# Self-attention of a decoder layer on one core: the order of copies and high parts, the place of the table steps, and the place of P's transposes are changed

## The chip, the cores and the metric

One core of one Trainium2 chip. The time is the device time of one execution in microseconds; before the change it was 1856.21 us, the median of three runs (1848.88 to 1856.5).

## The reference

A decoder layer on x (16 batches of 112 rows, 1024 wide) and a context (16 x 375 x 1024), float32: self-attention, cross-attention and a feed-forward part with 4-bit weights, each followed by a residual sum and a layer norm.

```python
# self-attention (width d = 256)
qkv = einsum('bsc,cf->bsf', x, Wqkv) + bqkv;  q, k, v = split(qkv)
attn = softmax(einsum('bqd,bkd->bqk', q, k) * d ** -0.5)
x = layernorm(x + einsum('bqd,dc->bqc', einsum('bqk,bkd->bqd', attn, v), Wo) + bo)
# cross-attention
Q = x @ Wq.T + bq;  K = ctx @ Wk.T + bk
x = layernorm(x + softmax(Q @ K.T / 32) @ ctx)
# feed-forward: W[k, n] = scales[g_idx[k], n] * (w4[k, n] - (z4[g_idx[k], n] + 1))
x = layernorm(x + (silu(x @ Wg) * (x @ Wu)) @ Wd)
```

## The kernel before

The kernel is written with one instruction list for each engine and hand-made semaphores; an engine takes its list in order, and a wait in it holds all that stands behind. Large products are made in float16 with a high and a low part of each operand: three passes (high x high, high x low, low x high). A high part is a scaled copy by ScalarE, a low part is the rest, by VectorE (GpSimd in some stages).

**Self-attention** (the first 255 us of the span) goes over 4 groups of 4 batches (rows 0 to 3 below, b in the code; S = 112 tokens each, a group is 448 columns). For a group g TensorE does, in order: four products for q and k (f = 0 to 3, 24 matmuls of 448 columns each, L1646 to L1650, into two banks of PSUM, so product f waits for the copy of f - 2); v of row 0 (24 matmuls of 256 columns); the scores of all four rows; v of rows 1, 2, 3; the transposes of P (L1671) when P is ready; the first half of the transposes of the next group's x (L1621); P times v; the second half; and the output product row by row. All products have the helper's line, L1628. In group 0 products 0 and 1 are L1641.

ScalarE copies q and k out of PSUM with scale and bias (L1356). From group 1 on the high part of the last row of the group before (`x1_hi`, L1350) stands between the copies of products 0 and 1; the high parts of rows 0 to 2 of a group stand at the group's end, so row 2's is ahead of the next group's copy of product 0. `x1_hi` waits for the normalised row and for the store of the slot's earlier row (two slots, stored by SP at L2045). Then come the exponentials (L1366), the high parts of the next x (L1344) and of the output's left operand (L1373).

VectorE: `x_max` of the next group (L490), the low part of the last row (L469), the group's entry of `beside`, then the maximum of the scores (L536), `x_factor` of the next group (L505 to L508, behind GpSimd's all-reduce L1154, which waits for `x_max`), the scaling of P (L543, L545), the two copies of v (L549, two rows each), the copy of P transposed (L554), low parts, and for each row the residual sum (L577), statistics and normalisation (L475).

The `beside` entries are the **table steps** for the feed-forward part: `table_rows` in group 1 (index rows, then numbers of rows and masks, L597 to L631), `table_parts` in group 2 (L636 to L666, scales split into three bfloat16 parts and zeros unpacked) and `select` in group 3 (L674 to L677). They are small steps with a semaphore wait after each. SP stores the tables (12 DMAs, L2093 to L2100) ahead of its part for the last group, and the selection (L2133) behind the first context's loads.

**Weight product** (about 240 to 351 us): M = Wq' Wk, 8 chunks of 32 float32 matmuls of 512 columns, 13.8 us each. ScalarE copies each chunk (L1401) and issues the load of the weights for a later one (L1400); GpSimd makes the bias terms (L1200 to L1210). TensorE's `largest_of_context(0)` (L1725) stands behind the sixth chunk. VectorE meanwhile: clears the padding of both context slots (L876), the maxima of context 0 (L772), `context_largest(0)` (L782, which waits for L1725), context 0's factor, the largest of m (L870), context 0's low parts (L803, behind ScalarE's high parts L1418), the maxima of context 1, the rest of m (L870), and, behind GpSimd's all-reduce L1242, the factors and low parts of M (L910), to which TensorE's L1810 is tied. SP's `next_ctx(1)` (L2117) waits for context 0's low parts; behind it stand the transposes of x1 and context 0 that cross-attention reads. The selection and the index rows lie in the memory of context slot 1.

Of the kernel before, what the change touches and what calls it, by code (L numbers as in the profile page):

```python
# [35 lines left out]
P = 128  # L36
# [4 lines left out]
def decoder_layer(nc, t_in, out):  # L41
    x_d, ctx_d = t_in["x"], t_in["ctx_4096"]
    NB, S, D = x_d.shape
# [7 lines left out]
    GB = 4  # L51
# [38 lines left out]
    with ExitStack() as ctx:  # L90
# [311 lines left out]
        def known(n, limit):  # L402

            return isinstance(n, int) and n < limit
# [38 lines left out]
        def _(dve):  # L443
# [82 lines left out]
            def self_attention(g, more, beside=()):  # L526
# [26 lines left out]
                dve.wait_ge(s_pt, g + 1)  # L553
                dve.tensor_copy(pt[0:S, :, :], bk[4][0:S, 0:TG].rearrange("p (b k) -> p b k", b=GB)).then_inc(s_pte, 1)  # L554
# [38 lines left out]
            def table_rows():  # L593
# [11 lines left out]
                T["idx"] = steps[0]  # L605

# [136 lines left out]
            self_attention(2, True, (table_parts,))  # L743
            self_attention(NG - 1, False, (select,))
# [130 lines left out]
            for i in range(2):  # L875
                dve.memset(cxp[i][96:P, CC - 1, :, :], 0.0)  # L876
# [4 lines left out]
            context_largest(0)  # L881
            context_factor(0, 0, False)
# [454 lines left out]
        def _(act):  # L1337
# [14 lines left out]
            def self_attention(g, more):  # L1352
                act.wait_ge(s_gf, 5 * g + 5)
                for f in range(2 * HC):
# [3 lines left out]
                    if f == 0 and not known(g, 1):  # L1358
                        x1_hi(g * GB - 1, GB - 1, 2 * g)
# [16 lines left out]
                for b in range(GB - 1):  # L1376
                    x1_hi(g * GB + b, b, 2 * g + b // 2 + 1)
# [232 lines left out]
        def _(pe):  # L1610
# [22 lines left out]
            def self_attention(g, more):  # L1633
# [30 lines left out]
                for b in range(1, GB):  # L1664
                    mm = v_rows(b)
                    if b % 2:
                        mm.then_inc(s_v, 1)
# [4 lines left out]
                mm.then_inc(s_pt, 1)  # L1672
                if more:
                    transposed_rows(g + 1, range(4))
# [334 lines left out]
        def _(sp):  # L2009
# [80 lines left out]
            sp.wait_ge(s_t, T["parts"])  # L2090
            for k in range(3):
                for m in range(2):
                    sp.dma_start(tabr_d[m, k * GU:(k + 1) * GU, :].rearrange("g n -> (g n)").rearrange("(p c) -> p c", p=P),  # L2093
                                 parts[:, k, at_fl[m]:at_fl[m + 1]]).then_inc(s_tabo, 16)
                sp.dma_start(dtab_d[k * GD:(k + 1) * GD, :].rearrange("g n -> (g n)").rearrange("(p c) -> p c", p=P),
                             parts[:, k, at_fl[2]:]).then_inc(s_tabo, 16)
            for m in range(2):
                sp.dma_start(tabr_d[m, 3 * GU:, :].rearrange("g n -> (g n)").rearrange("(p c) -> p c", p=64),
                             z_bf[0][64 * m:64 * m + 64, :]).then_inc(s_tabo, 16)
# [304 lines left out]
```

## Time and profile before

| | before |
|---|---|
| median of 3 runs, us | 1856.21 (1848.88 to 1856.5) |
| profiled execution, us | 1853.36 |
| its span, us | 1851.6 |
| TensorE busy | 1742.2 us, 94% |
| VectorE busy | 1064.8 us, 58% |
| ScalarE busy | 494.2 us, 27% |
| GpSimd busy | 500.9 us, 27% |

The span runs from the first to the last instruction; what the execution's time has beyond it lies around the program. A timeline lists instructions merged by line: start, duration, line, operation, shapes, count, and in brackets how long the engine was idle before and what released it. PE is TensorE, DVE VectorE, ACT ScalarE, POOL GpSimd, SPq the DMA queue of SyncE. Some matmul records are missing from the trace.

### The profile page before, as it was taken

To read this page: it belongs to the slowest core of one execution; us is meant where nothing else is said; L and a number is where in the kernel's file an instruction comes from. 1 tells how busy PE (TensorE), PEld (TensorE's weight loads), DVE (VectorE), ACT (ScalarE), POOL (GpSimd) and SP (SyncE) were. 2 spreads that over 40 slices of the span, in tenths; PEclk is the share of its full clock that TensorE was granted. 3 is DMA by queue.
4 is the path that set the end of the run, shared out by engine and by line. 5 is a ranking of instruction groups with operands and counts; after the bars stand their busy time and mean duration, and the time that the engine had idled before them with its cause. 6 is when DMAs were issued, how large, how long until landed. Compare 5 with 4: busy or idle time off the path is not lost.

```text
span 1851.6 us, 26675 instructions
## 1 busy us (share of the span) xinstructions
PE 1742.2 (94%) x9784; PEld 981.6 (53%) x9784; DVE 1064.8 (58%) x1656; ACT 494.2 (27%) x734; POOL 500.9 (27%) x326
## 2 busy tenths in 40 slices
PE   5898899898999969998999999999999899999998
PEld 3666644496787844444444444444445344444443
DVE  7788550666888856567778777777775111111011
ACT  3222210354555533232323223233232100000000
POOL 0322378223333425543322323223231000000000
PEclk9999999999999989999999999999999999999999
DMA  9342561599999975764231231322313822122120
GB/s 324 99 132 80 158 205 34 121 213 234 233 240 231 248 160 127 168 148 88 49 95 47 66 77 47 94 48 56 87 45 75 324 104 107 53 106 106 53 106 23
DMA packets 335590, 231.89 MB, mean 125 GB/s; under 512 B 288224, under 2 KB 302624, under 8 KB 333348
## 3 DMA queue, kind: packets, MB, share of 16 engines
q1 hardware_dynamic: 329284, 227.85, 47.2%
q10 hardware_dynamic: 6240, 3.15, 0.6%
q8 instruction: 43, 0.70, 0.2%
q14 instruction: 23, 0.19, 0.0%
HBM read 122.93 MB, written 60.83 MB: 99 GB/s over the span
## 4 chain that ended last, share of the span: by engine, by line
PE 47%; issue 27%; DVE 10%; DMA 6%; SPq 5%; POOL 2%; ACT 1%; DVEq 0%; POOLq 0%; ACTq 0%
PE psum L1628 45%; SPq L2143 4%; DMA arena<-arena 3%; DMA arena<-in_x 2%; DVE arena L803 1%; POOL small L1149 1%; POOL arena L1158 1%; PE psum L1839 1%; PE psum L1857 1%; DVE arena L974 1%; DVE arena L972 1%; DVE arena L969 1%; DMA x_parts_scratch<-arena 1%; DMA arena<-in_L_xattn_Wq 1%; DVE arena L993 1%
## 5 line engine op out<-in xcount | busy, mean ns | idle before, releaser
L1628 PE MATMUL psum<-arena 128*128 128x448 f16 (+5 forms) x7176 | 1276.7, 339 | 51.8 <-DMA arena<-arena 21.1
L1628 PEld LDWEIGHTS psum<-arena 128*128 128x128 f16 (+2 forms) x7176 | 753.6, 109 | 556.3 <-issue 97.2
L1967 PE MATMUL psum<-arena 128*128 128x512 f16 x1820 | 393.5, 379 | 6.2 <-DMA arena<-down_weights_scratch 3.7
L1967 PEld LDWEIGHTS psum<-arena 128*128 128x128 f16 x1820 | 177.6, 98 | 222.1 <-DMA arena<-down_weights_scratch 5.4
L1263 POOL TENSOR_TENSOR arena<-arena 128x1024 f16<-128x1024 f32 (+1 forms) x60 | 149.8, 2509 | 430.5 <-ACT arena L1494 430.5
L1131 DVE SCALAR_TENSOR_TENSOR arena<-psum,small,arena 128x512 f32<-128x512 f32 x28 | 20.9, 750 | 331.8 <-PE psum L1967 331.8
L1149 POOL TENSOR_TENSOR small<-small 112x1 f32<-112x1 f32 (+1 forms) x46 | 50.9, 1106 | 503.7 <-DVE small L464 503.7
L1494 ACT ACTIVATE arena<-arena 128x1024 f16<-128x1024 f32 (+1 forms) x60 | 68.8, 1173 | 128.2 <-DVE arena L955 99.8
L1508 ACT ACTIVATE arena<-arena,small 128x448 f32<-128x448 f32 x68 | 45.5, 668 | 208.6 <-DVE arena L1061 145.2
L1223 POOL TENSOR_TENSOR arena<-arena 128x224 f16<-128x224 f32 x64 | 54.8, 857 | 119.7 <-ACT arena L1412 119.6
L953 DVE TENSOR_TENSOR arena<-arena,psum 128x1024 f32<-128x1024 uint32 x65 | 79.1, 1217 | 2.9 <-PE psum L1839 0.9
L955 DVE TENSOR_TENSOR arena<-arena,psum 128x1024 f32<-128x1024 f32 x65 | 79.3, 1221 | 2.2
L1517 ACT ACTIVATE arena<-arena 128x448 f16<-128x448 f32 (+1 forms) x88 | 50.7, 576 | 106.8 <-DVE arena L982 106.8
L993 DVE TENSOR_TENSOR arena<-arena 128x448 f16<-128x448 f32 (+1 forms) x88 | 57.7, 656 | 36.8 <-ACT arena L1517 36.8
L772 DVE TENSOR_REDUCE small<-arena 128x1 f32<-128x1024 f32 (+1 forms) x48 | 57.6, 1215 | 25.4 <-DMA arena<-in_ctx 25.2
L803 DVE SCALAR_TENSOR_TENSOR arena<-arena,small 128x1024 f16<-128x1024 f32 (+1 forms) x48 | 61.2, 1278 | 12.0 <-ACT arena L1418 12.0
L1418 ACT ACTIVATE arena<-arena,small 128x1024 f16<-128x1024 f32 (+1 forms) x48 | 51.8, 1138 | 47.8 <-DVE small L799 47.8
L459 DVE BATCH_NORM_STATS2 small<-arena 112x6 f32<-112x512 f32 (+1 forms) x92 | 58.8, 681 | 1.4 <-DVE small L799 1.1
L982 DVE SCALAR_TENSOR_TENSOR arena<-arena,small 128x448 f32<-128x448 f32 (+1 forms) x72 | 48.9, 680 | 13.4 <-ACT arena L1526 10.6
L475 DVE TENSOR_SCALAR arena<-arena,small 112x1024 f32<-112x1024 f32 (+1 forms) x46 | 40.4, 878 | 26.4 <-POOL small L1149 26.4
L1270 POOL TENSOR_TENSOR arena<-arena 128x1024 f16<-128x1024 f32 x21 | 44.8, 2133 | 39.9 <-ACT arena L1502 39.9
L933 DVE TENSOR_TENSOR arena<-arena,small 128x1024 uint32<-128x1024 uint32 x43 | 53.7, 1249 | 0.3
(213 smaller groups left out, 1208.5 us busy)
## 6 DMA issues: line engine op xcount, KB each, us to landing
h_scratch<-arena SPq DMA_DIRECT2D x84, 224.0 KB, 2.9
arena<-h_scratch SPq DMA_DIRECT2D x13, 1376.0 KB, 6.1
arena<-in_ctx SPq DMA_DIRECT2D x32, 512.0 KB, 5.3
arena<-in_x SPq DMA_DIRECT2D x32, 448.0 KB, 5.6
x_scratch<-arena SPq DMA_DIRECT2D x32, 448.0 KB, 3.4
arena<-x_scratch SPq DMA_DIRECT2D x32, 448.0 KB, 4.6
arena<-in_L_ffn_down_qweight SPq DMA_DIRECT2D x21, 512.0 KB
down_weights_scratch<-arena SPq DMA_DIRECT2D x20, 512.0 KB, 3.8
```

The costliest lines, as they stand in the source:

```text
L459: dve.bn_stats(st[0:n, 6 * h:6 * h + 6], y[:, h * HALF:(h + 1) * HALF]).then_inc(s_st, 1)
L772: ins = dve.tensor_reduce(cmx[0:CP[c], c:c + 1], cx[0:CP[c], c, :], AX.X, ALU.max, apply_absolute_value=True)
L803: dve.scalar_tensor_tensor(cxp[b % 2][0:CP[c], c, 1, :], cx[0:CP[c], c, :], fc[0:CP[c], b:b + 1], cxp[b % 2][0:CP[c], c, 0, :], ALU.mult, ...
L953: dve.tensor_tensor(w, w.bitcast(U32), zeros, ALU.subtract).then_inc(s_dq, 1)
L955: dve.tensor_tensor(w, w, scales, ALU.mult).then_inc(s_wf if done is None else done, 1)
L993: dve.tensor_tensor(h_st[0:n, 1, cols], h_f[0:n, :], h_st[0:n, 0, cols], ALU.subtract).then_inc(s_hl, 1)
L1149: pool.tensor_tensor(rstd[0:n, :], ve[0:n, :], mhalf[0:n, :], ALU.pow).then_inc(s_rstd, 1)
L1263: return pool.tensor_tensor(dst[:, :, 1, :], wf32[:, lo * HALF:hi * HALF].rearrange("p (c n) -> p c n", n=P), dst[:, :, 0, :], ALU.subtract)
L1494: return act.activation(wgu[s][:, lo * 4:hi * 4, 0, :], wf32[:, lo * HALF:hi * HALF].rearrange("p (c n) -> p c n", n=P), ACT.Identity)
L1628: mm = pe.matmul(out, a, r, start=(k == 0), stop=(k == len(pairs) - 1))
L1967: mm = pe.matmul(bk[2 * s + c], ht[s][:, i, a, :], weights_of(i, w, c), start=(i == 0 and (w, a) == PASSES[0]), stop=(i == NI - 1 and (w, ...
L2143: sp.dma_start_transpose(cxt[s].rearrange("p l k t -> p (l k) t")[:, :, c * P:(c + 1) * P], cxp[s][:, c, :, :].rearrange("p l d -> p (l d) ...
```

## The change

Four edits, all of order: (1) ScalarE's high parts of rows 2 and 3 stand behind the copies of products 0 and 1 of the next group, in the groups that have one; in the last group rows 0 to 2 stay where they were. (2) TensorE transposes P behind v of row 2, ahead of v of row 3; VectorE copies P transposed between its two copies of v. (3) `table_rows` is cut in two; its first part stays in group 1, its second part (`row_numbers`), `table_parts` and `select` go behind `context_largest(0)`, and the clearing of context slot 1 goes behind them. (4) SP's table stores go behind the first context's loads and the last row's store, ahead of the store of the selection. No computation is added or removed.

```diff
@@ -550,8 +550,10 @@
-                dve.wait_ge(s_pt, g + 1)
-                dve.tensor_copy(pt[0:S, :, :], bk[4][0:S, 0:TG].rearrange("p (b k) -> p b k", b=GB)).then_inc(s_pte, 1)
+                    if p == 0:
+                        dve.wait_ge(s_pt, g + 1)
+                        dve.tensor_copy(pt[0:S, :, :], bk[4][0:S, 0:TG].rearrange("p (b k) -> p b k", b=GB)
+                                        ).then_inc(s_pte, 1)
@@ -603,6 +605,8 @@
                 T["idx"] = steps[0]
+
+            def row_numbers():
@@ -740,8 +744,8 @@
             self_attention(1, True, (table_rows,))
-            self_attention(2, True, (table_parts,))
-            self_attention(NG - 1, False, (select,))
+            self_attention(2, True)
+            self_attention(NG - 1, False)
@@ -872,13 +876,17 @@
-            for i in range(2):
-                dve.memset(cxp[i][96:P, CC - 1, :, :], 0.0)
+            dve.memset(cxp[0][96:P, CC - 1, :, :], 0.0)
             factor_step(dve.memset(cmx, 0.0))
             factor_step(dve.memset(cmx[:, CC:], LOW))
             for c in range(CC):
                 context_max(0, c)
             context_largest(0)
+            row_numbers()
+            table_parts()
+            select()
+
+            dve.memset(cxp[1][96:P, CC - 1, :, :], 0.0)
             context_factor(0, 0, False)
@@ -1355,8 +1363,8 @@
-                    if f == 0 and not known(g, 1):
-                        x1_hi(g * GB - 1, GB - 1, 2 * g)
+                    if f < 2 and not known(g, 1):
+                        x1_hi(g * GB - 2 + f, GB - 2 + f, 2 * g)
@@ -1373,7 +1381,7 @@
-                for b in range(GB - 1):
+                for b in range(GB - 2 if more else GB - 1):
                     x1_hi(g * GB + b, b, 2 * g + b // 2 + 1)
@@ -1661,15 +1669,14 @@
                 mm.then_inc(s_s, 1)
-                for b in range(1, GB):
-                    mm = v_rows(b)
-                    if b % 2:
-                        mm.then_inc(s_v, 1)
+                v_rows(1).then_inc(s_v, 1)
+                v_rows(2)
                 pe.wait_ge(s_p, g + 1)
                 pe.wait_ge(s_ve, 2 * g + 1)
                 for b in range(GB):
                     mm = pe.transpose(bk[4][0:S, b * S:(b + 1) * S], pr[0:S, b, :], ident[0:S, 0:S])
                 mm.then_inc(s_pt, 1)
+                v_rows(3).then_inc(s_v, 1)
                 if more:
                     transposed_rows(g + 1, range(4))
                 pe.wait_ge(s_pte, g + 1)
@@ -2087,6 +2094,36 @@
             sp.dma_start(idx_w, idx_d[2 * D:].partition_broadcast(P)).then_inc(s_tin[1], 16)
+            self_attention(NG - 1, False, False)
...
+            next_ctx(0)
+            store_parts(NB - 1, (NB - 1) % 2)
             sp.wait_ge(s_t, T["parts"])
             for k in range(3):
                 for m in range(2):
@@ -2099,36 +2136,6 @@
                          z_bf[1]).then_inc(s_tabo, 16)
-            self_attention(NG - 1, False, False)
...
-            next_ctx(0)
-            store_parts(NB - 1, (NB - 1) % 2)
             sp.wait_ge(s_t, T["sel"])
```

## Rows read from the trace of the kernel before

**Rows 1.** TensorE's timeline, 40 to 260 us: start, duration, line, operation, count [idle before <- releaser]

```profile
63.80 0.57 PE L1671 MATMUL psum<-ident,arena 112*112 112x112 f32 x4 [1.85 <-DVE arena L549]
...
94.78 22.87 PE L1628 MATMUL psum<-arena 128*128 128x448 f16 x160 [4.54 <-ACT arena L1356]
...
117.86 1.95 PE L1621 MATMUL psum<-ident,arena 112*128 112x112 f32 x16
...
172.39 0.59 PE L1671 MATMUL psum<-ident,arena 112*112 112x112 f32 x4 [3.67 <-DVE arena L549]
...
172.82 3.01 PE L1621 MATMUL psum<-ident,arena 112*128 112x112 f32 x16
...
201.31 4.71 PE L1628 MATMUL psum<-arena 128*128 128x448 f16 x24 [0.99 <-ACT arena L1356]
...
207.22 16.77 PE L1628 MATMUL psum<-arena 128*128 128x448 f16 x136 [1.20 <-ACT arena L1356]
```

**Rows 2.** ScalarE's timeline, 60 to 420 us

```profile
93.05 1.06 ACT L1350 ACTIVATE arena<-arena 112x1024 f16<-112x1024 f32 x1 [4.86 <-DMA x_parts_scratch<-arena]
```

**Rows 3.** VectorE's timeline, 40 to 270 us

```profile
61.39 0.15 DVE L505 TENSOR_SCALAR small<-small 128x1 f32<-128x1 f32 x1 [4.28 <-POOL small L1154]
...
114.33 0.62 DVE L545 TENSOR_TENSOR arena<-arena,small 112x448 f32<-112x448 f32 x1
...
150.03 4.41 DVE L490 TENSOR_REDUCE small<-arena 112x1 f32<-112x4096 f32 x1
...
167.73 0.62 DVE L536 TENSOR_REDUCE small<-psum 112x4 f32<-112x448 f32 x1
...
170.35 1.32 DVE L545 TENSOR_TENSOR arena<-arena,small 112x448 f32<-112x448 f32 x1
```

**Rows 4.** GpSimd's timeline, 60 to 420 us

```profile
109.26 0.38 POOL L1154 PARTITION_ALL_REDUCE small<-small  x1 [11.29 <-issue]
...
160.81 0.82 POOL L1154 PARTITION_ALL_REDUCE small<-small  x1 [11.55 <-issue]
...
168.86 2.33 POOL L1158 TENSOR_TENSOR arena<-arena 112x1024 f32<-112x1024 f32 x1 [7.22 <-issue]
...
328.01 1.90 POOL L1200 TENSOR_TENSOR arena<-arena,small 128x1024 f32<-128x1024 f32 x1 [4.61 <-DMA arena<-in_L_xattn_Wq]
...
334.88 2.35 POOL L1210 TENSOR_TENSOR arena<-arena 128x1024 f32<-128x1024 f32 x1
```

**Rows 5.** VectorE's timeline, 216 to 375 us

```profile
324.01 0.29 DVE L782 TENSOR_REDUCE small<-psum 128x1 f32<-128x128 f32 x1 [57.89 <-PE psum L1725]
...
339.92 3.67 DVE L803 SCALAR_TENSOR_TENSOR arena<-arena,small 128x1024 f16<-128x1024 f32 x3 [9.46 <-ACT arena L1418]
...
350.54 2.27 DVE L870 TENSOR_REDUCE small<-arena 128x1 f32<-128x2048 f32 x1
```

**Rows 6.** Windows of VectorE: stretch, length, busy (instructions), clock, DMA share, GB/s

```profile
155.40:167.73 12.33, 10.57 (x43) 1.00 0.00 1
...
106.53:111.70 5.17, 3.88 (x30) 1.00 0.02 3
...
sum 20.46, DVE 17.20; mean DVE 5.73
```

**Rows 7.** SP's queue, timeline of DMA issues, 60 to 400 us

```profile
211.21 0.90 SPq L2093 DMA_DIRECT2D table_scratch<-arena  x2
...
216.76 0.58 SPq L2100 DMA_DIRECT2D down_table_scratch<-arena  x1
...
259.59 8.78 SPq L2135 DMA_DIRECT2D arena<-down_table_scratch  x1
```

**Rows 8.** DMA view of the stretch 254 to 272 us, its line of packets

```profile
DMA packets 5870, 5.06 MB, mean 281 GB/s; under 512 B 2982, under 2 KB 5030, under 8 KB 5869
```

**Rows 9.** TensorE's timeline, 250 to 420 us

```profile
268.56 55.20 PE L1628 MATMUL psum<-arena 128*128 128x512 f32 x128 [1.68 <-DMA arena<-in_L_xattn_Wq]
...
358.66 5.96 PE L1810 MATMUL psum<-arena 128*128 128x224 f16 x30 [3.30 <-DVE arena L910]
```

More of the change, by code:

```diff
@@ L2089, in _ @@
             sp.dma_start(idx_w, idx_d[2 * D:].partition_broadcast(P)).then_inc(s_tin[1], 16)
[L2090 to L2099, printed above, removed]
-            sp.dma_start(dtab_d[3 * GD:, :].rearrange("g n -> (g n)").rearrange("(p c) -> p c", p=P),
-                         z_bf[1]).then_inc(s_tabo, 16)
             self_attention(NG - 1, False, False)
@@ L2131, in _ @@
             store_parts(NB - 1, (NB - 1) % 2)
+            sp.wait_ge(s_t, T["parts"])
+            for k in range(3):
+                for m in range(2):
+                    sp.dma_start(tabr_d[m, k * GU:(k + 1) * GU, :].rearrange("g n -> (g n)").rearrange("(p c) -> p c", p=P),
+                                 parts[:, k, at_fl[m]:at_fl[m + 1]]).then_inc(s_tabo, 16)
+                sp.dma_start(dtab_d[k * GD:(k + 1) * GD, :].rearrange("g n -> (g n)").rearrange("(p c) -> p c", p=P),
+                             parts[:, k, at_fl[2]:]).then_inc(s_tabo, 16)
+            for m in range(2):
+                sp.dma_start(tabr_d[m, 3 * GU:, :].rearrange("g n -> (g n)").rearrange("(p c) -> p c", p=64),
+                             z_bf[0][64 * m:64 * m + 64, :]).then_inc(s_tabo, 16)
+            sp.dma_start(dtab_d[3 * GD:, :].rearrange("g n -> (g n)").rearrange("(p c) -> p c", p=P),
+                         z_bf[1]).then_inc(s_tabo, 16)
             sp.wait_ge(s_t, T["sel"])
```

## The prediction

> **What bounds the kernel now.** Read the timeline of TensorE over self-attention first. It is nearly solid, so the time of this stage is its work plus the few gaps. The change aims at these: 4.54 us ahead of group 1's third q/k product, 0.99 and 1.20 us in group 3, both behind ScalarE's copy L1356, and 3.67 us ahead of group 2's transposes of P [rows 1]. ScalarE's timeline says why the first is there: the high part of row 2 (L1350) stands ahead of the copy, and itself waited 4.86 us for the store of row 0 [rows 2]. VectorE's timeline says why the last is there: in group 2 the maximum of the scores (L536) begins only at 167.73, behind the table steps [rows 3], though the scores were ready near 161 (v's products ended at 172.39 - 3.67 = 168.7, and three of them, 7.8 us, stand behind the scores). That gap costs more than its length: after it 16 transposes took 3.01 us, where 1.95 is usual [rows 1], as TensorE was granted 1.2 GHz there instead of 2.4.
>
> Then read what P itself needs. After the maximum VectorE takes `x_factor`, whose L505 waits for GpSimd's all-reduce: in group 0 for 4.28 us, to 61.39 [rows 3]. In groups 1 and 2 the all-reduce begins at 109.26 and 160.81 [rows 4], in group 2 6.4 us after x_max ended (L490, 150.03 and 4.41 us [rows 3]). It is hidden now, and is what is late next.
>
> Times below are on the clock of the trace before; a shift is carried to the next group, as each group starts behind the normalisation of the last one.
>
> **Copies ahead of high parts.** Nothing is added. The copy of product 0 no longer stands behind row 2's high part, nor that of product 1 behind row 3's. Products 2 and 3 then run without a gap. In group 3 this is 0.99 + 1.20, about **-2.1 us**: P waits for no all-reduce there, and the new order of v's products is neutral (the copy of P is hidden, but v's last copy now ends where P's did). In groups 1 and 2 the all-reduce cuts the gain short, next.
>
> **P transposed inside v's products.** The same matmuls in another order. One row's v is 24 of them, about 2.6 us (136 in 16.77 less 24 in 4.71 leaves 12.1 for four rows of v and some 1.6 of scores [rows 1]). Before, three rows of v covered the softmax; now two do (5.2 us), and the third comes after the transposes of P, ahead of the next group's x transposes. If L505 is the late one, x transposes begin at L505 + 2.4 (61.39 to 63.80 in group 0 [rows 1, 3]) + 0.4 for P's transposes + 2.6 for v = L505 + 5.4.
> - Group 0: L505 stays at 61.39, as nothing ahead of it moved. TensorE was through with v at 63.80 - 1.85 = 61.95; it is now through with two rows of it at 59.3, waits 4.4 us and starts the x transposes at 66.8 instead of 64.2: **+2.6**. The gap of 3.67 was followed by the low clock, that of 1.85 was not; v's last row then runs partly at half speed, about **+1.5**. Bounds of both together 2.6 and 5.2; +4.1.
> - Group 1: scores near 104, table rows to 106.5 (their second half begins there [rows 6]), L505 at 109.26 + 0.38, x transposes at 115.1 against 117.86: -2.75. The new gap of 2.9 us lies between the two above; I take half of 1.5 for the clock: **-2.0** (bounds -1.25, -2.75).
> - Group 2: the table steps are gone, scores near 157.5, L505 at 160.81 + 0.4, x transposes at 166.7 against 172.8: -6.1, and the 1.1 us of slow transposes goes: **-7.2** (bounds -6, -7.6).
>
> **Table steps moved.** They go behind `context_largest(0)`. VectorE's long idle stretch in the weight product, 57.89 us, ends *in* that step: L782 waits for TensorE's L1725, which comes behind six of eight chunks, and runs at 324.01 [rows 5]. VectorE takes its queue in order, so the moved steps begin at 324.3, after the hole and not in it. What is left behind it is 9.46 us ahead of L803 [rows 5]. Into this go `row_numbers` (5.17), `table_parts` (12.33) and `select`, 20.46 together [rows 6], and the memset that now stands behind `select`, about 1.1 (estimate). 21.5 - 9.46 = **+12.0**. Queued behind these steps are context 0's factor and low parts and the maximum of m on VectorE, ScalarE's high parts and the copy of the last chunk, and SP's load of context 1.
>
> Beside them GpSimd adds and multiplies from 328.01 to 337.23 [rows 4]. The scaling of P (L545) took 1.32 us instead of 0.62 while GpSimd's add of 168.86 ran, and ended 0.5 us after it [rows 3, 4]: a wide VectorE step with both inputs in SBUF waited for it. The wide table steps would begin at 331.9. Let each wait for the GpSimd step then running and GpSimd take its next one in between: the three scalings start near 332.1, 332.9 and 335.1 and the first cast behind GpSimd's last step near 337.8, where it would be 333.0: **+4.8**. Bounds 0 (no wide step meets one) and 7 (GpSimd's work left at 330, all of it waited for).
>
> The Trainium skill, "SBUF — State Buffer", section "SBUF: two separate sides", speaks against this placement: it has an exclusive lock for the whole instruction between GpSimd and a VectorE step with two SBUF inputs. By that rule `table_parts`' one-column products wait too, which no row shows; the turns would then cost 5.5 us instead of 4.8, and the forecast would be 0.7 us later.
>
> **SP's queue.** The 12 table stores (211.21 to 217.34, 6.1 us [rows 7]), the store of the selection, the wait for all 12, the loads of tab_d and two residual loads now all lie ahead of `next_ctx(1)`. With parts ready near 346.5, the stores are issued by 352.6 and the selection's by 353.3, the last table store lands near 356 (estimate), and context 1 is issued near 358, when L803 (from 356.7) frees it anyway. The residual loads (448 KB each) are new ahead of it in the DMA engines, 3.2 us at 281 GB/s [rows 8]; of that I count **+0.9** beyond the 6.9 us from L803's end to the last maximum of context 1 (343.6 to 350.5 [rows 5]), as the rest fits between its three loads. But tab_d's load once held SP for 8.78 us behind the selection's store [rows 7], with 1.5 MB of context queued ahead of both; now only the store is. Bounds 0 and 5.3 us.
>
> From the maxima of context 1 on the chain is as before: maximum of m, all-reduce, factors, high part, and TensorE at 358.66, which now waits far longer than 3.30 us for it [rows 9]. TensorE's L1725 for context 1 and the small products of v2 and u also come behind these maxima now; they fit beside the 8.1 us that follow.
>
> **One gain on the side.** SP's store of the selection (704 KB) leaves the stretch in which ScalarE's first load of weights is on its way, for which TensorE waits 1.68 us [rows 9]. It was 2.5 us of traffic [rows 8]: **-1.7** (bounds 0, -1.7).
>
> **The sum.** +4.1 - 2.0 - 7.2 - 2.1 - 1.7 = -8.9 up to the end of the weight product; +12.0 + 4.8 + 0.9 = +17.7 behind it; net +8.8. The profiled execution took 1853.36 us (span 1851.6, and 1.8 around it), 2.9 under the median of the three runs, 1856.21, and inside their spread. Forecast: 1853.4 + 8.8 = **1862.2 us**.
>
> **Rivals.**
> 1. *SP's queue becomes the bound.* tab_d's load holds it as before, to 353.3 + 8.8 = 362.1; context 1 then lands about 4.5 us later: 1866.7. With the clock losses of groups 0 and 1 in full (+1.8) and the full 7 us of turns (+2.2) it would be 1870.7. For it: the 8.78 row. Against: less is queued ahead. It decides from the point where tab_d is issued later than 358. Chance 0.2.
> 2. *The turns with GpSimd are nearly free*, as the wide steps fall between its instructions: 4.8 us less, 1857.4; with the better bounds of groups 0 and 1 (-2.3), 1855.1. For: GpSimd works for 9 us only. Against: the L545 row. Chance 0.25.
> 3. *The moved steps cost nothing*, because what TensorE waits for at 358.66 isn't VectorE's chain, or because they run in the hole after all: only the gains are left, 1853.4 - 8.9 = 1844.5. For: VectorE is idle for most of the weight product. Against: the hole ends in L782, ahead of them in the queue. Chance 0.08.
>
> The forecast itself has 0.47. What a measurement of this kernel can tell from no change is about 0.5%, 9.3 us, and the forecast lies at that edge: half of its chance is put on each side. Faster 0.08; slower 0.20 + half of 0.47 = 0.44; same the rest, 0.48. The range goes from 1850 (case 2 with every gain at its best) to 1871.
>
> **What would show it.** Group 0: a gap of 4.4 us ahead of P's transposes and a low clock after it. Groups 1 and 2: no gap behind L1356, gaps of 2.9 and 0.8 us ahead of P's transposes, with L505 waiting for GpSimd. The gap ahead of the third chunk of the weight product gone. VectorE: table steps directly behind L782, no idle time ahead of L803. TensorE: 15 to 25 us of gaps between the weight product and the first product with M, with small products in them. I am wrong if these are under 8 us, if L782 runs before TensorE's six chunks are done, or if group 0 does not lose.

## The result and the profile after

| | before | after |
|---|---|---|
| median, us | 1854.07 (6 runs, 1848.88 to 1856.5) | 1866.44 (6 runs, 1862.27 to 1869.69) |
| profiled execution, us | 1853.36 | 1865.75 |
| its span, us | 1851.6 | 1864.0 |

The changed kernel takes 1.0067 times as long, with an interval of 1.0047 to 1.0087: 12.4 us slower. The forecast was 1862.2, with a range of 1850 to 1871. One later execution of the kernel before took 4698.54 us, in the slow state, and is left out of the median that e8_residual_late and e10_both_behind are set against.

From here on lines are those of the changed kernel. The ones that matter have moved: L1628 to L1636 (products), L1671 to L1677 (P's transposes), L1621 to L1629 (x transposes), L1725 to L1732 (the context's small transposes), L1810 to L1817 (first product with M), L782 to L786, L803 to L807. A fence of an experiment has that kernel's own line numbers.

Read TensorE first, as before. Its timeline over self-attention and the weight product, as in [rows 1, 9]:

```profile
64.19 0.96 PE L1677 MATMUL psum<-ident,arena 112*112 112x112 f32 x4 [4.64 <-DVE arena L549]
64.95 3.97 PE L1636 MATMUL psum<-arena 128*112 128x256 f16 x24
68.75 1.93 PE L1629 MATMUL psum<-ident,arena 112*128 112x112 f32 x16
...
82.90 30.39 PE L1636 MATMUL psum<-arena 128*112 128x512 f16 x196 [0.89 <-DVE arena L579]
114.47 0.59 PE L1677 MATMUL psum<-ident,arena 112*112 112x112 f32 x4 [1.18 <-DVE arena L549]
114.90 2.79 PE L1636 MATMUL psum<-arena 128*112 128x256 f16 x24
117.52 1.94 PE L1629 MATMUL psum<-ident,arena 112*128 112x112 f32 x16
...
163.40 0.60 PE L1677 MATMUL psum<-ident,arena 112*112 112x112 f32 x4 [1.31 <-DVE arena L549]
...
166.45 1.94 PE L1629 MATMUL psum<-ident,arena 112*128 112x112 f32 x16
...
218.42 93.11 PE L1636 MATMUL psum<-arena 128*112 128x512 f16 x240 [1.44 <-DVE arena L561]
311.37 0.38 PE L1732 MATMUL psum<-ident,small 128*128 128x128 f32 x2
...
360.08 0.77 PE L1732 MATMUL psum<-ident,small 128*128 128x128 f32 x2 [20.86 <-DVE small L781]
360.64 3.41 PE L1748 MATMUL psum<-ones,arena 128*128 128x1 f32 x16
...
369.03 0.73 PE L1817 MATMUL psum<-arena 128*128 128x224 f16 x6 [1.08 <-DVE arena L918]
```

The waits for ScalarE's copies are gone: each group is one run of products from 82.90, 131.70 and 180.63 on. The price of P's new place stands in group 0: 4.64 us idle, then a row of v in 3.97 us where 2.79 is usual. The x transposes begin at 68.75; before, 64.20 (63.80 and the four transposes ahead [rows 1]). In group 2 they begin at 166.45 instead of 172.82. At the weight product's sixth chunk TensorE is 12.2 us ahead (311.37, before 323.59). Then come 20.86 us without a product, and the first product with M starts at 369.03, 10.4 us *later* than the 358.66 of [rows 9].

VectorE's timeline behind the weight product, which answers to [rows 5, 6]:

```profile
311.79 0.29 DVE L786 TENSOR_REDUCE small<-psum 128x1 f32<-128x128 f32 x1 [56.64 <-PE psum L1732]
...
317.14 0.81 DVE L640 TENSOR_SCALAR small<-small 128x3 f32<-128x3 f32 x1
...
321.09 1.75 DVE L653 TENSOR_TENSOR small<-small 128x1 f32<-128x1 f32 x1
...
323.06 2.98 DVE L658 TENSOR_SCALAR arena<-arena,small 128x172 f32<-128x172 f32 x3
...
344.99 3.68 DVE L807 SCALAR_TENSOR_TENSOR arena<-arena,small 128x1024 f16<-128x1024 f32 x3
355.34 1.22 DVE L776 TENSOR_REDUCE small<-arena 128x1 f32<-128x1024 f32 x1 [6.67 <-DMA arena<-in_ctx]
```

and GpSimd beside it, as in [rows 4]:

```profile
316.03 1.90 POOL L1208 TENSOR_TENSOR arena<-arena,small 128x1024 f32<-128x1024 f32 x1 [4.20 <-DMA arena<-in_L_xattn_Wq]
...
320.93 1.89 POOL L1215 TENSOR_TENSOR arena<-arena,small 128x1024 f32 x1 [0.21 <-POOL arena L1213]
322.90 2.35 POOL L1218 TENSOR_TENSOR arena<-arena 128x1024 f32<-128x1024 f32 x1
```

The hole of VectorE (56.64 us) still ends in the step ahead of the moved ones, and there is no idle time ahead of L807 any more. Between the two lie the table steps, 20.5 us of them in [rows 6], in part stretched by turns with GpSimd: L640 ends at 317.95 and GpSimd's L1208 at 317.93; L653 ends at 322.84, L1215 at 322.82. L658's three instructions take 2.98 us, where 0.99 is their time without GpSimd. The last term is on the right of the last line: context 1 lands 6.67 us after VectorE was ready for it.

### The profile page after: what moved, and what is told of

Same layout as the page of the kernel before. It is cut to its first block, busy times and chain, and to the rows that moved or that the text cites. A ratio compares the mean times of both kernels' runs of the same rounds, so it can differ in the third digit from the quotient of the medians.

```text
span 1864.0 us, 26676 instructions
## 1 busy us (share of the span) xinstructions
PE 1745.0 (94%) x9784; PEld 983.9 (53%) x9784; DVE 1067.9 (57%) x1656; ACT 493.9 (26%) x734; POOL 499.1 (27%) x326
## 3 DMA queue, kind: packets, MB, share of 16 engines
q10 hardware_dynamic: 6240, 3.15, 0.6%
## 4 chain that ended last, share of the span: by engine, by line
PE 48%; issue 28%; DVE 10%; SPq 5%; DMA 5%; POOL 2%; ACT 1%; DVEq 0%; POOLq 0%; ACTq 0%
PE psum L1636 46%; SPq L2150 4%; DMA arena<-arena 3%; DMA arena<-in_x 1%; DVE arena L807 1%; PE psum L1846 1%; PE psum L1864 1%; POOL small L1157 1%; DVE arena L982 1%; DVE arena L980 1%; POOL arena L1166 1%; DVE arena L977 1%; DVE arena L1001 1%; DVE arena L918 1%; DVE arena L483 1%
## 5 line engine op out<-in xcount | busy, mean ns | idle before, releaser
L1636 PE MATMUL psum<-arena 128*128 128x448 f16 (+5 forms) x7176 | 1275.9, 339 | 41.2 <-DMA arena<-arena 23.1
L1636 PEld LDWEIGHTS psum<-arena 128*128 128x128 f16 (+2 forms) x7176 | 754.6, 109 | 543.4 <-issue 93.7
L1139 DVE SCALAR_TENSOR_TENSOR arena<-psum,small,arena 128x512 f32<-128x512 f32 x28 | 20.9, 751 | 331.9 <-PE psum L1974 331.9
L807 DVE SCALAR_TENSOR_TENSOR arena<-arena,small 128x1024 f16<-128x1024 f32 (+1 forms) x48 | 61.2, 1279 | 2.6 <-ACT arena L1426 2.5
L990 DVE SCALAR_TENSOR_TENSOR arena<-arena,small 128x448 f32<-128x448 f32 (+1 forms) x72 | 48.9, 680 | 13.4 <-ACT arena L1534 10.6
L941 DVE TENSOR_TENSOR arena<-arena,small 128x1024 uint32<-128x1024 uint32 x43 | 53.7, 1249 | 0.3
L1166 POOL TENSOR_TENSOR arena<-arena 112x1024 f32<-112x1024 f32 x16 | 39.9, 2494 | 51.8 <-issue 27.7
```

Of the source, the lines that this page charges most:

```text
L807: dve.scalar_tensor_tensor(cxp[b % 2][0:CP[c], c, 1, :], cx[0:CP[c], c, :], fc[0:CP[c], b:b + 1], cxp[b % 2][0:CP[c], c, 0, :], ALU.mult, ...
L1166: pool.tensor_tensor(xr[0:S, b % 2, :], xr[0:S, b % 2, :], bo_b[0:S, :], ALU.add).then_inc(s_xb, 1)
L1636: mm = pe.matmul(out, a, r, start=(k == 0), stop=(k == len(pairs) - 1))
```

## The experiments

Ten kernels ran. Two places of each trace sum them up: when TensorE reaches L1732 (so what self-attention cost), and how long it is from there to the first product with M. The median is set against the median of the kernel before in the same session (1852.57 for e1, e2, e4 and e6; 1854.31 for e3, e5, e7 and e9; 1852.63 for e8 and e10; 1854.07 for the changed kernel). In the diffs of this section most context is cut, and what stands in brackets is told in words.

| kernel | L1732 at | from there to L1817 | median, against before |
|---|---|---|---|
| before | 323.59 | 35.1 | |
| after | 311.37 | 57.7 | 1866.44, +12.4 |
| e1_hole | 313.50 | 35.0 | 1844.03, -8.5 |
| e5_tables | 317.21 | 57.3 | 1871.83, +17.5 |
| e6_ctx_first | 310.04 | 53.9 | 1862.52, +10.0 |
| e8_residual_late | 315.19 | 53.7 | 1863.01, +10.4 |
| e3_copies | 325.27 | 35.3 | 1853.65, -0.7 |
| e4_ptrans | 336.38 | 35.1 | 1862.18, +9.6 |
| e2_both_orders | 340.16 | 34.9 | 1869.51, +16.9 |
| e9_p_behind_v | 306.48 | 34.8 | 1835.78, -18.5 |
| e7_factor_behind_p | 305.00 | 35.0 | 1833.41, -20.9 |
| e10_both_behind | 305.70 | 35.1 | 1834.85, -17.8 |

The first column is from single executions, and differs by some us between executions of the same instructions; e8_residual_late shows where. The trace of e4_ptrans is of an execution of 1869.03 us, 6.9 above that kernel's median, those of e3_copies and e2_both_orders lie 4.8 and 2.9 above theirs; so these three first-column entries are high.

### Behind the weight product

**e1_hole**: the changed kernel, with the table steps ahead of the step that waits, so that they can use the hole.

```diff
+            row_numbers()
+            table_parts()
+            select()
+            dve.memset(cxp[1][96:P, CC - 1, :, :], 0.0)
             context_largest(0)
-            row_numbers()
-            table_parts()
-            select()
-            dve.memset(cxp[1][96:P, CC - 1, :, :], 0.0)
             context_factor(0, 0, False)
```

> The changed kernel with row_numbers, table_parts and select (and the clearing of context slot 1) ahead of context_largest(0) instead of behind it. Theory (the steps cost time only because they stand behind the wait for TensorE's sixth chunk): they run in VectorE's 57 us hole, the gap behind the weight product goes back to about 3 us, the 12.2 us gained up to its end stay: 22.6 us less than the changed kernel, 1843.8 us. Rival (what the steps cost is shared use with GpSimd and the DMA engines, wherever they stand in the weight product): GpSimd's bias steps and ScalarE's weight loads behind them slip, TensorE waits in the weight product, and half or more of the 22.6 us stays: 1852 us or more.

Measured: 1844.03 us, 0.9954 (0.9936 to 0.9971). Its VectorE timeline:

```profile
273.29 5.71 DVE L658 TENSOR_SCALAR arena<-arena,small 128x172 f32<-128x172 f32 x3
...
287.84 7.37 DVE L665 TENSOR_SCALAR arena<-arena 128x43 uint32<-128x43 uint32 x8
...
315.87 0.29 DVE L786 TENSOR_REDUCE small<-psum 128x1 f32<-128x128 f32 x1
...
329.83 3.68 DVE L807 SCALAR_TENSOR_TENSOR arena<-arena,small 128x1024 f16<-128x1024 f32 x3 [7.51 <-ACT arena L1426]
```

The whole loss behind the weight product, 22.6 us, is gone (35.0 against before's 35.1), with not a step less on VectorE. So it was the place of the steps in the queue, and TensorE's wait was for this chain. The hole was only just long enough: GpSimd is busy for 51.95 of the 58 us from 257 to 315, and the steps, 20.5 us in [rows 6], lasted from 257.34 to 314.95. L786 had been waiting for 2 us by then.

**e5_tables**: the kernel before, with the table steps and SP's stores moved as in the change, and the other two parts undone. The diff is against the changed kernel.

```diff
-                    if f < 2 and not known(g, 1):
-                        x1_hi(g * GB - 2 + f, GB - 2 + f, 2 * g)
+                    if f == 0 and not known(g, 1):
+                        x1_hi(g * GB - 1, GB - 1, 2 * g)
...
-                for b in range(GB - 2 if more else GB - 1):
+                for b in range(GB - 1):
...
-                v_rows(1).then_inc(s_v, 1)
-                v_rows(2)
+                for b in range(1, GB):
+                    mm = v_rows(b)
+                    if b % 2:
+                        mm.then_inc(s_v, 1)
                 [P's transposes; VectorE's copy of P goes back behind both copies of v]
-                v_rows(3).then_inc(s_v, 1)
```

> The kernel before with the table steps and SP's stores moved as in the change (behind context_largest(0)), both other orders undone. Theory: group 2 loses its 3.7 us gap and the low clock, 5.2 us; the weight load's 1.7 us go; the 22.6 us behind the weight product come: 15.7 us slower than before, 1868 us. Rival (most of the gain in self-attention comes from the table steps, about 9 us, as they also hold P in groups 1 and 3): 1864 us.

Measured: 1871.83 us, 1.0107 (1.008 to 1.0135), 17.5 us slower than before, where the theory had 15.7. Its part in self-attention is a gain of 6.4 us, its loss behind the weight product 22.2 us (57.3 against 35.1), as in the changed kernel. The tables alone are worse than the whole change: the two new orders, which come with a loss in the kernel before (below), take back 5 us once the tables are gone from self-attention.

**e6_ctx_first** and **e8_residual_late** ask what holds context 1's load. The first puts it ahead of the store of the selection, of tab_d and of the residual loads; the second moves only the residual loads.

```diff
+            next_ctx(1)                      # e6 only
             sp.wait_ge(s_t, T["sel"])
             sp.dma_start(seld_d ...)
             ...
-            for n in range(2):               # e8 only: behind next_ctx(1)
-                load_residual(n, n)
-            next_ctx(1)                      # e6 only
+            for n in range(2):               # e8 only
+                load_residual(n, n)
```

> The changed kernel with SP's load of context 1 ahead of the store of the selection, the loads of tab_d and the residual loads. Theory (context 1 landed 4.3 us late because 1.8 MB were ahead of it in the DMA engines, SP itself was free): VectorE's idle time ahead of context 1's maximum goes from 6.67 to about 2 us, 4.3 us less than the changed kernel, 1862 us. Rival (the landing is bound otherwise, as all of the traffic shares the engines in any order): 1866 us, same as the changed kernel.

> The changed kernel with only the two residual loads (448 KB each) put behind the load of context 1; the selection's store and tab_d's loads stay ahead. Theory (the 0.9 MB of residual rows were half of the 1.8 MB ahead of context 1): the 6.67 us wait ahead of context 1's maximum goes to about 4, 2.5 us less than the changed kernel, 1864 us. Rival (the store of the selection with its pieces of 256 bytes was what held the DMA engines): no change, 1866.5 us.

Measured: 1862.52 us, 1.0063 (1.0041 to 1.0084), and 1863.01 us, 1.0055 (1.0035 to 1.0075). By the medians this is 3.9 and 3.4 us less than the changed kernel, and 2.4 and 2.0 us less when each is set against the kernel before of its own session; the intervals overlap, so the traces have to carry it. SP's queue in the changed kernel, and the landing times of the DMA view from 340 to 360 us (issues, KB each, us from issue to landing):

```profile
340.78 0.43 SPq L2140 DMA_DIRECT2D down_selection_scratch<-arena  x1
342.10 1.84 SPq L2142 DMA_DIRECT2D arena<-down_table_scratch  x1
...
344.60 0.80 SPq L2104 DMA_DIRECT2D arena<-x_scratch  x2
346.31 1.55 SPq L2112 DMA_DIRECT2D arena<-in_ctx  x2
```

```profile
arena<-in_ctx SPq DMA_DIRECT2D x2, 512.0 KB, 9.3
arena<-x_scratch SPq DMA_DIRECT2D x2, 448.0 KB, 7.6
down_selection_scratch<-arena SPq DMA_DIRECT2D x1, 704.0 KB, 4.9
```

SP issued the context at 346.31, when the first of L807's three instructions was just through: nobody waited for SP. The load then took 9.3 us to land, where it took 4.5 us before. Ahead of it had gone the 704 KB of selection, which had landed by then (340.78 and 4.9), and the 896 KB of residual rows, issued at 344.60 and 7.6 us on their way. With the context first, or with the residual loads behind it, it lands in 4.6 and 4.2 us, and VectorE's wait for it shrinks from 6.67 us to 1.14 and 1.09 us. One line of each kernel:

```profile
348.59 1.22 DVE L776 TENSOR_REDUCE small<-arena 128x1 f32<-128x1024 f32 x1 [1.14 <-DMA arena<-in_ctx]
```

```profile
353.86 1.22 DVE L776 TENSOR_REDUCE small<-arena 128x1 f32<-128x1024 f32 x1 [1.09 <-DMA arena<-in_ctx]
```

A part of this comes back in the waits for the later pieces of context 1: all three waits together go from 7.41 us to 3.59 and 3.21. From L1732 to the first product with M both kernels save some 4 us. As moving the residual loads alone does it, and as SP issues the context 1.3 to 1.4 us behind L807's start in all three kernels, these 896 KB in the DMA engines are the cause, not SP's queue and not tab_d. The selection's store stays ahead in e8_residual_late and costs nothing that shows.

e8_residual_late also shows why single executions scatter. Its self-attention is the changed kernel's, and yet it reaches L1732 3.8 us later. The difference lies in a step that normalises x, and comes once in group 0 and once in group 1:

```profile
87.68 2.83 DVE L475 TENSOR_SCALAR arena<-arena,small 112x1024 f32<-112x1024 f32 x1 [0.45 <-POOL small L1157]
```

GpSimd's wide addition (L1166) started at 87.61 here and ran for 2.35 us, just ahead of the step, which took 2.83 us. In the profiled execution of the changed kernel the addition began at 88.76, just behind the step, which took 0.81 us. All that follows in the group is 2.0 us later or earlier by this. Over groups 0 and 1 the kernel before had one such meeting of 2.83 us in its profiled execution, the changed one and e6_ctx_first none, e8_residual_late and e2_both_orders two.

### Self-attention

**e3_copies**: the kernel before with the copies of q and k ahead of the high parts, and nothing else.

```diff
-                    if f == 0 and not known(g, 1):
-                        x1_hi(g * GB - 1, GB - 1, 2 * g)
+                    if f < 2 and not known(g, 1):
+                        x1_hi(g * GB - 2 + f, GB - 2 + f, 2 * g)
...
-                for b in range(GB - 1):
+                for b in range(GB - 2 if more else GB - 1):
```

> The kernel before with ScalarE's copies ahead of the high parts only. Theory (the table steps hold P in all three groups, so most of what the copies gain comes back as a gap ahead of P): group 1 -1.5, group 2 0, group 3 -2: 3.5 us faster than before, 1849 us. Rival (the copies' gaps are gained whole, 4.5 and 1.4 for the clock in group 1, 3.3 in group 2, 2.2 in group 3): 11 us faster, 1841 us.

Measured: 1853.65 us, 1.0004 (0.9985 to 1.0023): nothing, where the theory had 3.5 us. TensorE's timeline:

```profile
77.78 33.01 PE L1628 MATMUL psum<-arena 128*112 128x512 f16 x220 [0.89 <-DVE arena L577]
114.50 0.99 PE L1671 MATMUL psum<-ident,arena 112*112 112x112 f32 x4 [3.70 <-DVE arena L549]
...
173.59 1.00 PE L1671 MATMUL psum<-ident,arena 112*112 112x112 f32 x4 [9.02 <-DVE arena L549]
```

The gaps behind the copies did go (33.01 us in one run), and came back whole ahead of P: 3.70 us in group 1, where there was none, and 9.02 in group 2, where there were 3.67 [rows 1]. P is ready at a time that VectorE's queue sets, with the table steps in it; that time doesn't come earlier when q and k do.

**e4_ptrans**: the kernel before, with P transposed inside v's products, and nothing else.

```diff
-                for b in range(1, GB):
-                    mm = v_rows(b)
-                    if b % 2:
-                        mm.then_inc(s_v, 1)
+                v_rows(1).then_inc(s_v, 1)
+                v_rows(2)
                 [P's transposes]
+                v_rows(3).then_inc(s_v, 1)
```

> The kernel before with only P's transposes put inside v's products (and VectorE's copy of P between its copies of v). Theory (v's last row moves behind P, so wherever P is late the x transposes slip by a row of v): group 0 +2.3 at the next x_max, group 1 0, group 2 +2.6 and some for a low clock, group 3 +0.5: 6 us slower than before, 1860 us. Rival (the order pays by itself, as the copy of P is hidden): 1 us faster than before, 1853 us.

Measured: 1862.18 us, 1.0051 (1.0033 to 1.0069). The gaps ahead of P are 4.70, 0.87, 6.29 and 2.13 us, and behind the first and the third the row of v runs in 5.33 and 5.01 us instead of 2.79. The first:

```profile
63.20 0.97 PE L1671 MATMUL psum<-ident,arena 112*112 112x112 f32 x4 [4.70 <-DVE arena L549]
63.96 5.33 PE L1630 MATMUL psum<-arena 128*112 128x256 f16 x24
```

**e2_both_orders**: e3_copies and e4_ptrans together, the tables left where they were (both diffs above).

> The kernel before with both new orders (ScalarE's copies ahead of high parts, P's transposes inside v's products), the table steps left where they were. Theory (in groups 2 and 3 the table steps still hold P back, so the gaps gained at the copies come back ahead of P): group 0 +2.3, group 1 -2.6, group 2 +2.6, group 3 0: 2 us slower than before, 1856 us. Rival (the orders carry the 10 us gained in self-attention, the table steps were no part of it): 1844 us.

Measured: 1869.51 us, 1.008 (1.0058 to 1.0102), where my theory had 1856. I had priced the tables' hold on P in group 1 as a gain of 2.6 us and in group 2 as a loss of 2.6; the trace shows every group losing:

```profile
120.77 0.99 PE L1671 MATMUL psum<-ident,arena 112*112 112x112 f32 x4 [6.89 <-DVE arena L549]
121.56 3.80 PE L1630 MATMUL psum<-arena 128*112 128x256 f16 x24
...
183.42 0.99 PE L1671 MATMUL psum<-ident,arena 112*112 112x112 f32 x4 [13.41 <-DVE arena L549]
184.21 4.88 PE L1630 MATMUL psum<-arena 128*112 128x256 f16 x24
```

One row of v that stood ahead of P stands behind it, so the gap of e3_copies grows by that row and somewhat more (3.70 to 6.89, 9.02 to 13.41; a row of v is 2.79), and the row itself then runs in part at the low clock. Where P is late, its place inside v costs 17.6 us (+16.9 against the -0.7 of e3_copies); this is why the change needs its third part, the tables out of self-attention.

**e9_p_behind_v**: e1_hole with P's transposes and their copy behind all of v again, as before.

```diff
-                v_rows(1).then_inc(s_v, 1)
-                v_rows(2)
+                for b in range(1, GB):
+                    mm = v_rows(b)
+                    if b % 2:
+                        mm.then_inc(s_v, 1)
                 [P's transposes]
-                v_rows(3).then_inc(s_v, 1)
```

> As e1_hole, but with P's transposes behind all of v's rows, and the copy of P behind both copies of v, as in the kernel before: so copies ahead of high parts, and table steps in the hole. Theory (P waits for GpSimd's all-reduce and comes later than v's third row in group 0 and about with it in groups 1 and 2, so the new place of P only puts a row of v behind it): x transposes begin 4.2 us earlier in group 0, of which some 2 are left behind its normalisations, 1.0 in group 1 and 1.2 in group 2: 4 us less than e1_hole, 1840 us. Rival (P inside v hides the copy of P and pays): 2 us more than e1_hole, 1846 us.

Measured: 1835.78 us, 0.9911 (0.9884 to 0.9938). The second part of the change, in the kernel as it would be with the tables in the hole, costs 8 us by the medians and 10 when each is set against its own session (7.0 us in the traces, at L1732); the theory had 4. What is left ahead of P are 2.23 us in group 0 and 0.95 in group 2.

**e7_factor_behind_p** leaves P where the change put it and takes away what P waits for: `x_factor`, with its wait for the all-reduce, goes behind the scaling of P, the first copy of v and the copy of P.

```diff
-                if more:
-                    x_factor(g + 1)
                 dve.wait_ge(s_exp ...)
                 ...
                     if p == 0:
                         [copy of P]
+                        if more:
+                            x_factor(g + 1)
```

> As e1_hole (P inside v), but VectorE takes the next group's x_factor, which waits for GpSimd's all-reduce, behind the scaling of P, the first copy of v and the copy of P. Theory (the all-reduce is what holds P): TensorE's gaps ahead of P's transposes (3.2, 3.1 and 1.4 us in e1_hole) go, and the low clock after them: 5 us less than e1_hole, 1839 us; VectorE's and ScalarE's parts of the next x are not late, as the factor is there when the x transposes are. Rival (the factor is needed as early as P: ScalarE's high parts of x wait for it and TensorE for them): same as e1_hole, 1844 us.

Measured: 1833.41 us, 0.9894 (0.9867 to 0.9921), the lowest median of all. TensorE:

```profile
59.62 0.57 PE L1677 MATMUL psum<-ident,arena 112*112 112x112 f32 x4 [0.62 <-DVE arena L547]
60.02 2.79 PE L1636 MATMUL psum<-arena 128*112 128x256 f16 x24
...
109.28 0.59 PE L1677 MATMUL psum<-ident,arena 112*112 112x112 f32 x4 [1.61 <-DVE arena L547]
```

This is 10.6 us less than e1_hole, twice the 5 us of the theory. The gaps of e1_hole ahead of P (3.18, 3.09 and 1.38 us) have become 0.62, 1.61 and none, 5.4 us less, and the low clock behind the second of them, where P and the row of v took 0.99 and 5.33 us instead of 0.59 and 2.79, is gone: another 2.9 us. At L1732 the two traces are 8.5 us apart. So what held P, once its cover was gone, was this one wait, L505 for GpSimd, which didn't have to stand ahead of P at all.

**e10_both_behind**: e9_p_behind_v and the factor behind P's copy.

```diff
-                if more:
-                    x_factor(g + 1)
                 ...
                 [copy of P, behind both copies of v]
+                if more:
+                    x_factor(g + 1)
```

> As e9_p_behind_v (P's transposes behind all of v, table steps in the hole), with x_factor behind the scaling of P, the copies of v and the copy of P, as in e7. Theory (with P no longer behind the all-reduce the place of its transposes is worth nothing, except that v's third row covers the 1.6 us gap that e7 still has in group 1, where the index steps hold the maximum): e7 less 1.6 us, 1831.8 us. Rival (P inside v pays once P is in time, as it hides the copy of P and that of v): 2 us more than e7, 1835.5 us.

Measured: 1834.85 us, 0.9904 (0.989 to 0.9919). TensorE has no gap ahead of P in any group, where e7_factor_behind_p had 0.62 and 1.61 us, and the times are the same within what was measured; neither the theory's 1.6 us less nor the rival's 2 us more can be told from it. With the wait out of P's way no difference shows between the two places of P's transposes. Nor does one show between this kernel and e9_p_behind_v (1835.78), which has the wait in its old place: behind all of v, P was late by 2.23 us at most. So one of the two moves is enough, P behind v or the factor behind P.

## Why the prediction was right, and where it wasn't

The prediction had a loss behind the weight product that is larger than the gain ahead of it, and that is what happened: +22.6 and -12.2 us, forecast +17.7 and -8.9. The two errors, 4.9 and 3.3 us, partly cancel, and that the total came within 4.2 us is in part luck. By its own steps:

| step | forecast | measured |
|---|---|---|
| group 0 | +4.1 | +4.5, of which 2.1 came back |
| group 1 | -2.0 | -2.7 |
| group 2 | -7.2 | -7.4 |
| group 3 | -2.1 | -2.6 |
| weight load | -1.7 | -1.7 |
| steps behind the hole, less the idle time | +12.0 | +12.0 |
| turns with GpSimd | +4.8 | +5.2 |
| context 1's landing | +0.9 | +4.3 |
| small products | 0 | +1.1 |

**Copies and P.** The chain named was the right one: P waits for VectorE's L549, which waits for L505, which waits for GpSimd's all-reduce. In the changed kernel:

```profile
61.77 0.15 DVE L505 TENSOR_SCALAR small<-small 128x1 f32<-128x1 f32 x1 [4.45 <-POOL small L1162]
...
112.14 0.15 DVE L505 TENSOR_SCALAR small<-small 128x1 f32<-128x1 f32 x1 [2.39 <-POOL small L1162]
...
161.08 0.15 DVE L505 TENSOR_SCALAR small<-small 128x1 f32<-128x1 f32 x1 [3.36 <-POOL small L1162]
```

Group 0's gap was to be 4.4 us and was 4.64; the slow row was to cost 1.5 and cost 1.2 (3.97 less 2.79). e7_factor_behind_p shows the cause by taking the wait out. What stands ahead of that all-reduce in group 0 the prediction left unsaid, and it isn't `x_max`, which had ended at 42.58:

```profile
44.88 0.35 POOL L1183 PARTITION_ALL_REDUCE small<-small  x1 [33.39 <-DVE small L700]
52.39 3.12 POOL L1166 TENSOR_TENSOR arena<-arena 112x1024 f32<-112x1024 f32 x1 [7.16 <-issue]
61.36 0.38 POOL L1162 PARTITION_ALL_REDUCE small<-small  x1 [5.86 <-issue]
```

GpSimd's queue has the addition of the output bias (`add_bo(0, 0)`, L1166) between two all-reduces. Putting it behind the second one may take away group 0's wait; no run tried it.

The gaps of groups 1 and 2 were to be 2.9 and 0.8 us and were 1.18 and 1.31; both errors are within the 2 us by which the normalisation of x scatters (in e8_residual_late the gaps are 3.12 and 3.53). The 2.1 us that came back in group 0 go with such a meeting as well: its L475 took 2.83 us in the profiled execution of before and 0.81 in that of after. As e8_residual_late meets it in the same order of instructions, I take it for chance and not for an effect of the change, though one trace of each kernel doesn't show that. Without it the first five terms give -10.1.

**Table steps.** +12.0 to a tenth: VectorE takes its queue in order, and the hole ends in the step ahead. e1_hole proves it by swapping the two. The turns with GpSimd were forecast as 4.8 us, with 5.5 by the rule of the Trainium skill ("SBUF — State Buffer", "SBUF: two separate sides"), and are 5.2 (`table_parts` took 17.5 us, 12.33 in [rows 6]). That 4.8 came so close is in part luck: it was worked out for the three wide scalings alone, and L658 has only 2.0 of the loss. The other 3.4 us lie in four narrow steps ahead of it (L640, L643, L646, L653), which the forecast had as free. What I took from [rows 3, 4] was that wide steps wait. The trace shows that one-column products wait too (L653, 1.75 us instead of 0.16), and so does a scaling of three columns, L640. In the same page of the Trainium skill, section "Who interferes with whom", `tensor_scalar`, `copy` and `cast` are among the steps that can take the pair of ports shared with GpSimd, under conditions; L640 agrees. One-column `tensor_scalar` steps were not held, though: L644 took 0.15 us at 319.33, in the midst of GpSimd's L1213. So the Trainium skill covers the one-column products, which my reading of the rows left out.

**SP's queue.** Rival 1 had tab_d's load hold SP for 8.78 us as before; it held it for 1.84, and SP was never late. The step that failed is the price of the residual loads in the DMA engines: +0.9 us in the sum, 4.3 measured. I worked it out as 3.2 us of traffic at 281 GB/s and let most of it fit between the context's three loads: +0.9. But the first of these loads is the one that is queued behind all of it, and nothing of VectorE's work can start without it. The bound of 5.3 us held it; the value should have been taken near that end.

**Small products.** I had them fit beside the 8.1 us from the last maximum to the first product with M; it took 9.2. They come behind 20.86 us without work, at half of TensorE's clock: in the windows (us, busy time of PE, PEld, DVE, ACT, POOL, granted clock, DMA share, GB/s)

```profile
342.00:344.00 2.00, 0.00 (x0) 0.00 (x0) 2.00 (x1) 1.60 (x2) 0.00 (x0) 0.96 1.05 219
344.00:346.00 2.00, 0.00 (x0) 0.00 (x0) 1.96 (x2) 0.00 (x0) 0.00 (x0) 0.50 0.94 185
```

the clock is 1.2 GHz from 344 us on. L1748's 16 products then take 3.41 us, before 1.84, and VectorE's L901 waits 0.96 us for what comes out of them. I had counted the idle time and left out what it does to the next piece of work, though the forecast had charged just that in group 0.

**Rivals 2 and 3** are out: the turns weren't free, and nothing ran in the hole. Rival 3's reason, that VectorE is idle for most of the weight product, is sound for another order of the queue: e1_hole.

From the first product with M on the changed kernel loses another 2.0 us (12.4 in all, 10.4 by then). I have no cause for it and leave it open. No kernel touches this stage; from its first exponential to its last it took 290.6 us in the kernel before, 294.2 in the changed one, and 291.1 to 294.3 in the ten others.

**How the parts work together.** Alone, each part gives nothing or a loss: copies -0.7, P +9.6, tables +17.5 us. With all three it is +12.4 and not their sum, 26.4, because what the first two do depends on the third. As long as table steps hold P, an earlier q or k only makes TensorE wait longer at P, and one row of v less ahead of P adds to that wait.

## What to carry to other kernels

Work that is moved "into an idle stretch" has to stand in the queue ahead of the wait in which this stretch ends: here the place of one call decides between +12.4 and -8.5 us. Before taking cover from ahead of a wait, list what the covered operand needs on its own engine; if a step for later work stands in that chain with a wait in it (here `x_factor`), move that step first. And a load that the next stage starts with is priced by its landing time behind everything issued ahead of it, so what isn't urgent goes behind it.

## What the runs showed of the hardware

Small VectorE steps beside a busy GpSimd were much dearer than I had thought. In e1_hole L665's eight instructions of 43 columns took 7.37 us, in the changed kernel beside an idle GpSimd 1.89; all the table steps took 57.6 instead of 20.5 us. In these 57.6 us VectorE ran 79 instructions and GpSimd 36, so at most every second step can have lost its turn to a GpSimd instruction. Which ones did is uneven: one-column `tensor_scalar` steps kept their 0.15 us, while a step of two columns (L633) took 2.19 instead of 0.17.

The low clock after a gap was less regular than I had it. Gaps ahead of P of 4.63 us and over were always followed by it. Between 3.09 and 3.70 us both happened: after 3.12, 3.18 and 3.53 us P's transposes took 0.57 to 0.60 us and what came behind them was fast too, after 3.09, 3.39 and 3.70 us they took 0.97 to 1.00, and after the 3.67 us of the kernel before they took 0.59 and the clock fell to 1.2 GHz just behind them. Gaps of 2.23 us and under were not followed by it, with one exception: in group 3 of e3_copies three short gaps came close together (0.77, 0.72 and 1.44 us), and the 16 products between the last two took 3.15 us instead of 2.04, at 1.2 GHz from 226 us on.

In groups 1 and 2 the all-reduce of GpSimd begins some 6 us after VectorE's maximum: L490 ends at 105.49 and 154.14 in the changed kernel, and the all-reduces start at

```profile
111.73 0.38 POOL L1162 PARTITION_ALL_REDUCE small<-small  x1 [11.41 <-issue]
...
160.67 0.38 POOL L1162 PARTITION_ALL_REDUCE small<-small  x1 [11.70 <-issue]
```

It works for 0.38 us. This is no fixed delay behind the maximum: in group 0 the all-reduce begins 5.86 us after GpSimd's own addition, and behind the weight product, where GpSimd had been idle for 39.78 us, it begins 0.14 us after the step that releases it. What GpSimd does in the time ahead of it the profile doesn't show, and it wasn't tried.
